# Block map of 64 segments in a routed-experts kernel: the expert loop awaits the rows of three token groups instead of four

## The reference

```
h = layernorm(x) * (1 + ca) + sa
x = x + ga * linear_attention(h)            # 8 heads of 32
h = layernorm(x) * (1 + cb) + sb
scores = sigmoid(h @ w_router)              # 32 experts
idx = top6 of (scores + bias), within the 4 best of 8 groups of experts
routed = sum over the 6 chosen e of scores[e] * (silu(h @ gate[e]) * (h @ up[e])) @ down[e]
shared = (silu(h @ sh_gate) * (h @ sh_up)) @ sh_down
x = x + gb * (routed + shared)
```

## Time and profile before

| | |
|---|---|
| times of the runs | 577.68, 585.07, 584.3 us; median 584.3 |
| profiled execution | 584.41 us |
| its span, first to last instruction | 582.6 us |
| mean granted TensorE clock | 0.889 |
| PE busy | 472.4 us (81%) |
| DVE, ACT, POOL busy | 232.7, 176.3, 284.2 us |
| DMA packets | 83.25 MB, mean 143 GB/s |

### The profile page before, as it was taken

One profiled execution on the slowest core, in us unless ns is written; L12 is line 12 of the kernel. 1 busy time (PEld: TensorE's weight loads), 2 busy tenths in 40 slices (PEclk: granted clock), 3 DMA queues, 4 the chain that ended last, 5 costly groups with the idle time before them and its releaser, 6 DMA issues.

```text
span 582.6 us, 9494 instructions
## 1 busy us (share of the span) xinstructions
PE 472.4 (81%) x1994; PEld 325.4 (56%) x1995; DVE 232.7 (40%) x983; ACT 176.3 (30%) x429; POOL 284.2 (49%) x253
## 2 busy tenths in 40 slices
PE   4898989827785459829699999999999999999800
PEld 3455755417534216415477777777777777777600
DVE  2726789405871027301133334334333333333206
ACT  2231322201220003001144444444444444444300
POOL 2303512770777731760045655665666666655630
PEclk9799978967895759958899999999999999999865
DMA  8999010330458842841257766567665757677459
GB/s 282 342 333 380 31 73 24 124 124 11 152 143 270 282 162 83 292 168 61 67 89 108 111 96 109 101 108 105 113 105 103 109 94 114 105 117 110 52 131 334
DMA packets 87922, 83.25 MB, mean 143 GB/s; under 512 B 22522, under 2 KB 80348, under 8 KB 87901
## 3 DMA queue, kind: packets, MB, share of 16 engines
q1 hardware_dynamic: 66012, 52.59, 31.1%
q0 software_dynamic: 19584, 28.33, 26.2%
q10 hardware_dynamic: 2304, 2.10, 1.1%
HBM read 43.13 MB, written 40.90 MB: 144 GB/s over the span
## 4 chain that ended last, share of the span: by engine, by line
PE 72%; issue 10%; DVE 7%; another core or an unknown queue 4%; DMA 4%; ACT 2%; SPq 1%; POOL 0%; POOLq 0%; ACTq 0%; DVEq 0%
PE bank L1444 21%; PE bank L1459 16%; PE bank L1361 8%; PE bank L1372 5%; PE bank L1437 4%; PE bank L1452 4%; PE bank L1261 4%; PE bank L1247 2%; PE bank L1334 2%; PE bank L1163 2%; DMA token_sums<-tok_buf,dest 1%; DMA XH<-in_L_attn_x 1%; PE bank L1280 1%; PE bank L1195 1%
## 5 line engine op out<-in xcount | busy, mean ns | idle before, releaser
L592 POOL DMA_INDIRECT token_sums<-tok_buf,dest x104 | 161.9, 1557 | 138.2 <-ACT tok_buf L775 52.2
L1444 PE MATMUL bank<-gate_up,tok_buf 128*128 x416 | 142.7, 466 | 0.4 <-DVE tok_buf L1109 0.4
L564 POOL DMA_INDIRECT pair_rows<-XH,rows_i x96 | 94.6, 985 | 62.7 <-DVE rows_i L1028 34.3
L1109 DVE COPY tok_buf<-bank 128x256 f32<-128x256 f32 x104 | 44.2, 425 | 172.2 <-PE bank L1437 143.8
L1459 PE MATMUL bank<-down,tok_buf 88*128 x416 | 109.9, 387 | 0.0
L1444 PEld LDWEIGHTS bank<-gate_up,tok_buf 128*128 128x128 f32 x416 | 80.0, 193 | 29.4 <-issue 2.1
L1459 PEld LDWEIGHTS bank<-down,tok_buf 88*128 88x128 f32 x416 | 71.0, 191 | 7.7 <-issue 0.2
L775 ACT ACTIVATE tok_buf<-bank,tok_buf 128x256 f32<-128x256 f32 x104 | 49.2, 473 | 55.0 <-PE bank L1459 28.7
L1361 PE MATMUL bank<-tok_buf,sh_gu 128*128 128x512 f32 (+1 forms) x96 | 50.1, 673 | 10.8 <-issue 10.8
L760 ACT ACTIVATE tok_buf<-bank 128x176 f32<-128x176 f32 x104 | 33.0, 317 | 79.9 <-PE bank L1444 73.3
L1437 PEld LDWEIGHTS bank<-ident,tok_buf 128*128 128x128 f32 x208 | 27.3, 141 | 37.9 <-issue 29.7
(11 more groups left out here) (153 smaller groups left out, 462.6 us busy)
## 6 DMA issues: line engine op xcount, KB each, us to landing
tok_buf<-pair_rows SPq DMA_DIRECT2D x104, 128.0 KB
gate_up<-in_L_ffn_gate_w SPq DMA_DIRECT2D x8, 704.0 KB, 8.5
gate_up<-in_L_ffn_up_w SPq DMA_DIRECT2D x8, 704.0 KB, 9.1
down<-in_L_ffn_down_w SPq DMA_DIRECT2D x2, 2816.0 KB
pair_rows<-sh_rows SPq DMA_DIRECT2D x1, 5120.0 KB, 18.9
gate_up<-token_sums SPq DMA_DIRECT2D x16, 256.0 KB, 6.0
XH<-in_L_attn_x SPq DMA_DIRECT2D x4, 512.0 KB, 9.7
token_sums<-sh_rows ACTq DMA_DIRECT2D x16, 128.0 KB
```

The source lines that it names most:

```text
L564: nc.gpsimd.indirect_dma_start(out=pair_rows, out_offset=bass.IndirectOffsetOnAxis(ap=rows_i[:, t, k:k + 1], axis=0), in_=XH[:, t, :], in_ ...
L592: nc.gpsimd.indirect_dma_start(out=token_sums[c % 2], out_offset=bass.IndirectOffsetOnAxis(ap=dest[:, c:c + 1], axis=0), in_=yw[:, c, :], ...
L1109: V.tensor_copy(xT[:, c % 2], banks[0][:, 0:C].rearrange("p (k n) -> p k n", k=KC)).then_inc(xT_copied, 1)
L1444: last = mm(banks[1 + c % 2][:, 0:M2], xT[:, c % 2, k, :], gate_up[:, bass.ds(e * (KC * M2) + k * M2, M2)], start=k == 0, stop=k == KC - 1)
```

## The change

The map has 64 segments instead of 32. Segment e of the first 32 holds the full blocks of expert e that the tokens of the first three groups fill (`used_first`, a copy of the counts taken after the third group). Segment 32 + e holds the expert's other blocks. The count of blocks is the same, and each block's rows are the same; the order is another, and every expert is visited twice. The dispatches of the fourth group count on a semaphore of their own. SP awaits the first 72 (`FIRST_PAIRS`) ahead of the loop and the other 24 behind its second turn, and its first two turns are written out instead of one. POOL issues 29 dispatches ahead of the deviations of group 1,0 instead of 25, and up to n = 33 instead of 31 ahead of those of group 1,1.

```diff
@@ -40,6 +40,8 @@
     TURNS = -(-NBLK // 4)
     FEWEST = T * TOPK // P // 4 - 1
     MAP_W = P + 8
+    FIRST_PAIRS = (NT - GT) * TOPK
+    assert FIRST_PAIRS - E * (P - 1) // P > 3 * 4
     XW = C + 2 * E
     REC = E + 1
     PAIR_ROWS = T * E
@@ -107,6 +109,7 @@
         minus_half = sb("minus_half", [P, TB])
         modT = sb("modT", [P, 4, B])
         mapf = sb("mapf", [P, 5])
+        which = sb("which", [P, 2])
         block = sb("block", [P, 3])
 
 
@@ -143,7 +146,8 @@
         ones_bf = part(P // 2).bitcast(bf16)
         weighed = part(GT * TOPK * E).rearrange("p (i k e) -> p i k e", i=GT, k=TOPK)
         more = part(E * NT).rearrange("p (e n) -> p e n", e=E)
-        seg = part(4 * E).rearrange("p (a e) -> p a e", a=4)
+        seg = part(12 * E).rearrange("p (a h e) -> p a h e", a=6, h=2)
+        used_first = part(E)
         iota_n = part(NT)
         bias_bc = part(E)
         stats = part(NT * 6).rearrange("p (i k) -> p i k", i=NT)
@@ -194,7 +198,8 @@
             sem(n) for n in ("csB_ready", "gated_projection_ready", "keys_values_used"))
         var2_ready, rstd2_ready, h2_ready = (sem(n) for n in ("var2_ready", "rstd2_ready", "h2_ready"))
         divided, shares_stored = sem("x1_divided"), [sem(f"x1_shares_stored{g}") for g in range(NT // GT)]
-        sel_ready, recs_ready, dispatched = (sem(n) for n in ("chosen_ready", "rows_ready", "rows_dispatched"))
+        sel_ready, recs_ready = sem("chosen_ready"), sem("rows_ready")
+        dispatched, last_dispatched = sem("first_rows_dispatched"), sem("last_rows_dispatched")
         zeros_ready, heads_clear = sem("zeros_ready"), sem("segment_heads_clear")
         dest_ready = sem("destinations_ready")
         sh_stored = [sem(f"shared_rows_stored{s}") for s in range(2)]
@@ -370,14 +375,15 @@
                 skip_runtime_bounds_check_because="the map's entries are clamped where they are made")
             return values
 
-        def blocks(eng, step):
+        def blocks(eng, step, fixed=1):
 
 
 
 
             last_turn = load_last_turn(eng)
-            step(0, False)
-            with eng.Fori(1, FEWEST) as turn:
+            for turn in range(fixed):
+                step(turn, False)
+            with eng.Fori(fixed, FEWEST) as turn:
                 step(turn, False)
             with eng.Fori(0, (TURNS - FEWEST) // 2) as two:
                 turn = two * 2 + FEWEST
@@ -443,7 +449,7 @@
             load_gate_up(EARLY, E, ld_late)
 
             await_read(sp, ("map",))
-            sp.wait_ge(dispatched, 16 * NT * TOPK)
+            sp.wait_ge(dispatched, 16 * FIRST_PAIRS)
 
             def load_rows(c, col):
                 sp.dma_start(xg[:, c, :], pair_rows[bass.DynSlice(col, P, E), 0:C]).then_inc(x_loaded[c], 16)
@@ -470,8 +476,10 @@
                         if not isinstance(n, int) or n + 1 >= R:
                             sp.wait_ge(dest_ready, n + 2 - R)
                         load_records((c + 1) % R, cols[c + 1])
-
-            last_turn = blocks(sp, step)
+                if isinstance(turn, int) and turn == 1:
+                    sp.wait_ge(last_dispatched, 16 * (NT * TOPK - FIRST_PAIRS))
+
+            last_turn = blocks(sp, step, 2)
 
             def fetch_sums(a, g):
                 t = g * OT
@@ -563,17 +571,17 @@
                     pool.wait_ge(recs_ready, t // GT + 1)
                     nc.gpsimd.indirect_dma_start(
                         out=pair_rows, out_offset=bass.IndirectOffsetOnAxis(ap=rows_i[:, t, k:k + 1], axis=0),
-                        in_=XH[:, t, :], in_offset=None).then_inc(dispatched, 16)
+                        in_=XH[:, t, :], in_offset=None).then_inc(dispatched if n < FIRST_PAIRS else last_dispatched, 16)
 
 
             second_deviation(0, 0)
             second_deviation(0, 1)
             pool.wait_ge(heads_clear, 16)
-            dispatch(0, 25)
+            dispatch(0, 29)
             second_deviation(1, 0)
-            dispatch(25, 32)
+            dispatch(29, 34)
             second_deviation(1, 1)
-            dispatch(32, NT * TOPK)
+            dispatch(34, NT * TOPK)
 
 
             for g in range(NT // GT):
@@ -1051,29 +1059,47 @@
             second_norm(1, 1)
             hidden(0, 0)
             records(1, 0)
+            V.tensor_copy(used_first, used[:, :])
             choose(1, 1)
             hidden(0, 1)
             records(1, 1)
 
 
 
+            counts, ends, offsets, hot, part_of, ones = (seg[:, a] for a in range(6))
+
+            def flat(ap):
+                return ap.rearrange("p h e -> p (h e)")
+
+            full_blocks = (FIRST_PAIRS // TOPK) + 1
+            shape = [P, E, full_blocks - 1]
+            link(V.tensor_tensor(more[:, :, 1:full_blocks], used_first.unsqueeze(2).broadcast_to(shape),
+                                 iota_n[:, 1:full_blocks].unsqueeze(1).broadcast_to(shape), ALU.is_ge))
+            link(V.tensor_reduce(counts[:, 0], more[:, :, 1:full_blocks], AX.X, ALU.add))
             shape = [P, E, NT]
             link(V.tensor_tensor(more, used[:, :].unsqueeze(2).broadcast_to(shape),
                                  iota_n[:, :].unsqueeze(1).broadcast_to(shape), ALU.is_gt))
-            link(V.tensor_reduce(seg[:, 0, :], more, AX.X, ALU.add))
-            link(V.memset(seg[:, 2, :], 1.0))
-            link(V.tensor_tensor_scan(seg[:, 1, :], seg[:, 2, :], seg[:, 0, :], 0.0, ALU.mult, ALU.add))
-            link(V.tensor_tensor(seg[:, 0, :], seg[:, 1, :], seg[:, 0, :], ALU.subtract))
-
-            link(V.tensor_scalar(seg[:, 2, :], seg[:, 1, :], iota_p[:, 0:1], None, ALU.is_le))
-            link(V.tensor_reduce(mapf[:, 0:1], seg[:, 2, :], AX.X, ALU.add))
-            link(V.tensor_scalar(mapf[:, 0:1], mapf[:, 0:1], float(E - 1), None, ALU.min))
-
-            link(V.tensor_scalar(seg[:, 3, :], iota_e[:, :], mapf[:, 0:1], None, ALU.is_equal))
-            link(V.tensor_tensor(seg[:, 0, :], seg[:, 3, :], seg[:, 0, :], ALU.mult))
-            link(V.tensor_reduce(block[:, 0:1], seg[:, 0, :], AX.X, ALU.add))
-            link(V.tensor_tensor(seg[:, 3, :], seg[:, 3, :], used[:, :], ALU.mult))
-            link(V.tensor_reduce(block[:, 1:2], seg[:, 3, :], AX.X, ALU.add))
+            link(V.tensor_reduce(counts[:, 1], more, AX.X, ALU.add))
+            link(V.tensor_tensor(counts[:, 1], counts[:, 1], counts[:, 0], ALU.subtract))
+            link(V.memset(ones, 1.0))
+            link(V.tensor_tensor_scan(flat(ends), flat(ones), flat(counts), 0.0, ALU.mult, ALU.add))
+            link(V.tensor_tensor(flat(offsets), flat(ends), flat(counts), ALU.subtract))
+            link(V.tensor_tensor(offsets[:, 1], offsets[:, 1], counts[:, 0], ALU.subtract))
+
+            link(V.tensor_scalar(flat(hot), flat(ends), iota_p[:, 0:1], None, ALU.is_le))
+            link(V.tensor_reduce(which[:, 0:1], flat(hot), AX.X, ALU.add))
+            link(V.tensor_scalar(which[:, 0:1], which[:, 0:1], float(2 * E - 1), None, ALU.min))
+            link(V.tensor_scalar(which[:, 1:2], which[:, 0:1], -float(E), None, ALU.add))
+            link(V.tensor_scalar(mapf[:, 0:1], which[:, 1:2], 0.0, float(E), ALU.is_lt, ALU.mult))
+            link(V.tensor_tensor(mapf[:, 0:1], mapf[:, 0:1], which[:, 1:2], ALU.add))
+
+            for h in range(2):
+                last = V.tensor_scalar(hot[:, h], iota_e[:, :], which[:, h:h + 1], None, ALU.is_equal)
+            link(last)
+            link(V.tensor_tensor(flat(part_of), flat(hot), flat(offsets), ALU.mult))
+            link(V.tensor_reduce(block[:, 0:1], flat(part_of), AX.X, ALU.add))
+            link(V.tensor_tensor(hot, hot, used[:, :].unsqueeze(1).broadcast_to([P, 2, E]), ALU.mult))
+            link(V.tensor_reduce(block[:, 1:2], flat(hot), AX.X, ALU.add))
             link(V.tensor_scalar(block[:, 0:1], iota_p[:, 0:1], block[:, 0:1], float(P), ALU.subtract, ALU.mult))
             link(V.tensor_scalar(block[:, 2:3], block[:, 1:2], -float(P), 0.0, ALU.add, ALU.max))
             link(V.tensor_tensor(block[:, 2:3], block[:, 2:3], block[:, 0:1], ALU.min))
@@ -1081,9 +1107,9 @@
             V.tensor_tensor(mapf[:, 4:5], block[:, 1:2], block[:, 2:3], ALU.subtract)
             link(V.scalar_tensor_tensor(out=mapf[:, 1:2], in0=block[:, 2:3], scalar=float(E), in1=mapf[:, 0:1],
                                         op0=ALU.mult, op1=ALU.add))
-            link(V.tensor_scalar(seg[:, 3, 0:TURNS], iota_e[:, 0:TURNS], float(R), None, ALU.mult))
-            link(V.tensor_scalar(seg[:, 3, 0:TURNS], seg[:, 3, 0:TURNS], seg[:, 1, E - 1:E], None, ALU.is_lt))
-            link(V.tensor_reduce(mapf[:, 2:3], seg[:, 3, 0:TURNS], AX.X, ALU.add))
+            link(V.tensor_scalar(ones[:, 0, 0:TURNS], iota_e[:, 0:TURNS], float(R), None, ALU.mult))
+            link(V.tensor_scalar(ones[:, 0, 0:TURNS], ones[:, 0, 0:TURNS], ends[:, 1, E - 1:E], None, ALU.is_lt))
+            link(V.tensor_reduce(mapf[:, 2:3], ones[:, 0, 0:TURNS], AX.X, ALU.add))
```

## The result

| | before | after |
|---|---|---|
| median of the runs | 583.05 us (20 runs, 576.62 to 586.49) | 587.51 us (20 runs, 580.9 to 591.59) |
| ratio to before | | 1.0073, 95% interval 1.0044 to 1.0102 |
| profiled execution | 584.41 us, span 582.6 | 585.16 us, span 583.4 |
| mean granted clock | 0.889 | 0.885 |

The forecast was 582.5 us; the kernel did not become a little faster but a little slower. A second comparison of the same two kernels, on another occasion, gave 585.92 against 585.21 us, ratio 1.0002 (0.9958 to 1.0045). So the loss is between nothing and 0.7%. What both agree on is that the earlier dispatches and the shorter wait of SP bought nothing.

A forecast was written before the change was run, and what follows sets the result against it. The prediction took PE and its gaps as the bound, with the ends of POOL's dispatch bursts setting the path from 98 to 264 us. -3.0 + 1.2 = -1.8 us on 584.41 gave 582.6, stated as 582.5; range 574 to 591.

The forecast's parts named there:

- part 4: POOL's moved dispatches, the only part said to touch the path: first burst costs 1.2 us, earlier release gains 3.0.
- Part 1: SP's wait ahead of the loop: passed at some 245 us instead of 263.7, worth 0; second wait holds nothing.
- Part 4, first burst: Four more dispatches in POOL's first burst prolong PE's late results: cost 1.2 us, bounds 0 and 5.1.
- the slower rival: Longer first burst holds attention of batch 1 for the full 5.1 us, row loads add 1.5: 588 us; chance 0.19.
- Part 4, the release: Second burst with 43 dispatches instead of 47 releases ACT 2.9 to 3.7 us earlier; 3.0 taken, lower bound 0.
- The rival of the break: New break at 174.8 in the second burst lets PE's results out: 579 us, chance 0.20; whole hold gone, 0.04.
- Part 3: Longer map on DVE: 2.75 us more, hidden behind PE's hidden layer; cost 0, bounds 0 and +0.6.
- Part 2: Four early row loads on SP's queue fall into the third burst: cost 0 taken, up to 1.5 us.
- Part 5: The loop: as many blocks and turns, same last blocks, so the tail stays; 0, bounds -1 and +1.

The follow-up runs named there:

- q3: The changed kernel with an awaited 128-column memset ahead of dispatches 72 to 95 only, which thins the third burst; 565.46 us, ratio 0.9654.
- e2: The kernel before with only the two places changed at which dispatches are interrupted, 29 and 34 instead of 25 and 32; 586.88 us, ratio 1.0014.
- e1: The changed kernel with only the 64-segment map left: old dispatch boundaries, one wait for all 96 ahead of the loop; 586.57 us, ratio 1.0121.
- p2: The changed kernel with two awaited memsets of 192 columns ahead of each dispatch, 1.84 us apart; 566.7 us, ratio 0.9818.
- e6: The changed kernel with one dispatch in flight, each awaiting the one ahead of it; 735.82 us, ratio 1.2703.
- e8: The changed kernel with dispatch 72 held back until the last shared row has been read; 586.42 us, ratio 1.0148.
- e3: The changed kernel with the dispatches interrupted at the old boundaries, 25 and 32; 588.9 us, ratio 1.0083.
- e4: The changed kernel with both of SP's waits ahead of the loop and one turn written out; 584.92 us, ratio 0.9992.
- q5: The kernel before with nine linked memsets in the map's chain on DVE, 1.35 us in all; 588.91 us, ratio 1.0058.
- p1: The changed kernel with an awaited 128-column memset ahead of each dispatch, 1.47 us apart; 532.95 us, ratio 0.9237.
- q2: The changed kernel with an awaited 128-column memset ahead of each dispatch and both of SP's waits ahead of the loop; 548.79 us, ratio 0.9396.
- e5: The kernel before with one dispatch in flight, each awaiting the one ahead of it; 753.67 us, ratio 1.3028.

## Why the prediction was wrong

- **The step that failed** is the sentence that ends part 4: the third burst begins when group 1,1's rows are ready, "which follows that release; all behind it moves along". The release came 27.5 us earlier and the burst 4.2 (the sum had 3.0 less 1.2, so 1.8). What is behind the burst did not move along: entry followed 59.0 us behind its start instead of 54.2, and these 4.8 us took the gain back. In before one shared row passed in the middle of the third burst; the prediction took for granted that it still would. After, the map's result came out 15 us late, and all shared rows of group 1,0 waited for the burst's end. q3 shows the price: with that burst thinned, entry follows 38.0 us behind its start. Why more was held is shown only in part: PE came to the map at +14.0 us instead of +11.4, and the map was longer. e2 has only the first of the two, e1 only the second, and each had the long hold.
- **Part 1**: its time failed by that same mechanism. SP was to pass soon after the map, at some 245 us. It did when the third burst was thinned (247.6), but with the dense one the map's result itself was held and SP passed at 258.48. Its worth, 0, was right, and the second wait cost nothing, in p2 too. What part 1 didn't see is that POOL's scatters stand behind all 96 dispatches: e6, e8 and p2 show that this queue, not SP's, limits how far an early entry can pay.
- **Part 4, first burst**: sized at 1.2 us with an upper bound of 5.1. The traces say 4.8. Attention was held for the whole extension, as the slower rival had it. The second burst ended 6.0 us later instead of 3.7 earlier, since group 1,0's rows were ready at 186.09 instead of 176.43.
- **Part 4, the release**: the reason given (an earlier end of burst or traffic) was wrong, though the sign was right. The new break runs from 180.52 to 186.37, and ACT's wait ahead of the router of group 1,1 ended at 182.61 within it; the router's result followed at 187.47. The rival of the break foretold that. Its payoff did not come, as the hold then fell on the hidden layer (9.05 and 7.84 us) and on the third burst. Nor is the break shown to be needed: the second trace of before had the result at 185.22 without it.
- **Part 3** was right in size (2.46 us for 2.75) and in that PE comes to the map no later for it (+11.4 in e1, e3 and e4, as in before). Its cost of 0 is not borne out: with the longer map and the old boundaries, e1 and e3 entered 58.6 and 59.5 us behind the burst's start. The sum of part 3 asked only whether PE would wait for DVE, and not whether the later map and weights would meet the hold. q5 had half of the delay and no long hold. **Part 2** never came to the test in after, since the loads of rows started behind the third burst. In p1 they started inside it (215.98), and the dispatches went on each 1.47 us and the last began at nearly the same time as in q2, at 241.78 and 241.29; both are 33.73 us behind the burst's start. The Trainium skill's rule ("DMA: Bandwidth & Descriptors", SWDGE vs HWDGE vs iDMA), by which early loads take turns with dispatches, thus cost nothing that shows in when the dispatches were issued.
- **Part 5** was right: 274.3 us from entry to the last scatter against 274.7, tail 24.7 against 24.1.
- **The slower rival** gave 588 us, next to what was measured. Its first half (the whole extension lost) is shown. Its second half, that the loss is carried through to the end, is not: e2, which has that loss alone, comes to 1.0014, and in after the third burst began earlier all the same.
- **What stays open**: why the runs of the first comparison lie 0.7% above before and those of the second do not, while the profiled executions differ by 0.75 us. How a dense burst delays PE's results and, at times, PE itself. And by which way the longer map leads into the long hold.

## What to carry to other kernels

If results come late without a releaser while another engine issues DMAs in a row, first thin out that row and measure. Here an added 0.2 us for each of 96 dispatches made the kernel 4.4% faster, and only then was the shortened wait worth its 16 us (by the medians and the entry in the traces). When you shift a stretch that blocks others, don't carry the rest along by the same amount: ask of each later event whether it falls before, into or behind the stretch. And where a wait is moved behind a loop's entry, look at every queue on which the loop's own work stands behind what was awaited.

## What the runs showed of the hardware

- A dense run of indirect DMAs of GpSimd (128 rows of 1280 bytes, one each 1.26 us) holds back what PE has finished. The waiting engine gets it up to 29 us late (the router's result in before: PE's last matmul ended at 185.62, ACT took it at 214.94; in after the map's result was 15 us late). In before and after the holds begin some 10 to 16 us into a burst and end 2 to 5 us behind the start of its last dispatch. It is no count of dispatches: e5 issues as many without holds. It is no DMA of the waiting engine either: ACT also awaits its own stores ahead of a shared row, but for the 10.83 us until 260.83 the last of them had moved by 236 us, and DVE's wait for the map has no DMA in it.
- It depends sharply on spacing: at 1.26 us long holds, at 1.37 us "remote" waits of ACT of up to 13 us, at 1.47, 1.84 and 3.25 us none over 3 us. The share in which the DMA engines are busy does not decide it (0.33 with holds in the first burst of before, 0.89 without in p1). The mechanism was not found.
- After such holds PE ran slower: 20 matmuls of L1398 took 7.67 us, where 24 of the same line took 5.54 at 275.50. The clock granted was 0.50 (1.2 GHz, the lower of its two levels) from 216 to 226 us and 1.00 (2.4 GHz) from 230 to 240; PE had stood idle for 11.61 us before.
